# Residual block of two 3x3 convolutions on one core: F(4,3) over ten tiles in two groups, another order of the products, planes made one image further ahead

## What is computed

```python
out = conv3x3(x, lsq_quantize(w1, alpha1))      # pad 1, stride 1, 128 -> 128 channels
out = relu(batchnorm(out, gamma1, beta1))       # mean and variance over batch, rows, columns
out = conv3x3(out, lsq_quantize(w2, alpha2))
out = batchnorm(out, gamma2, beta2)
out = relu(out + x)
```

## Time and profile before

| what | value |
|---|---|
| median of 3 runs | 1474.97 us (1474.01 to 1475.03) |
| the profiled execution: time, span | 1474.11 us, 1472.3 us |
| mean granted TensorE clock | 0.89 |
| PE matmul busy | 1132.3 us, 77% |
| DVE busy | 1145.5 us, 78% |
| ACT busy | 854.4 us, 58% |
| POOL busy | 462.5 us, 31% |

### The profile page before, as it was taken

The page is one execution under the profiler, slowest core; times in us unless marked ns, Lnnn a source line. Parts: engine busy times, 40 slices in busy tenths (PEclk is TensorE's granted clock), DMA queues, the critical chain, the costliest instruction groups (busy, mean ns, idle before and its releaser), DMA issues.

```text
span 1472.3 us, 19175 instructions
## 1 busy us (share of the span) xinstructions
PE 1132.3 (77%) x5802; PEld 1030.9 (70%) x5802; DVE 1145.5 (78%) x1562; ACT 854.4 (58%) x1263; POOL 462.5 (31%) x211
## 2 busy tenths in 40 slices
PE   5999999999999998899999999999999400000000
PEld 5999999999999997899999999999999400000000
DVE  8999999999999996988888888888888642223324
ACT  3655555655565556677777777777777532322224
POOL 3444444444444552433334333333333100000000
PEclk9999999999999999899999999999999755555555
DMA  4454454444452210022245455444230799999999
GB/s 163 157 191 188 189 193 174 174 174 174 174 191 106 96 44 0 0 89 87 93 186 196 184 194 191 179 174 174 87 131 16 277 429 430 431 429 429 430 429 409
DMA packets 28098, 296.83 MB, mean 202 GB/s; under 512 B 3888, under 2 KB 3888, under 8 KB 4912
## 3 DMA queue, kind: packets, MB, share of 16 engines
q1 hardware_dynamic: 22608, 245.25, 42.2%
q10 hardware_dynamic: 5472, 51.38, 8.2%
HBM read 174.59 MB, written 122.03 MB: 201 GB/s over the span
## 4 chain that ended last, share of the span: by engine, by line
issue 52%; POOL 26%; DMA 18%; DVE 1%; ACT 1%; POOLq 1%; ACTq 0%; DVEq 0%
POOL v_lo L417 26%; DMA slots<-conv_spill 11%; DMA out<-slots 4%; DMA xbuf<-in_x 3%; DVE slots L860 1%; ACT slots L611 1%; POOLq L422 1%; POOLq L416 0%; POOLq L77 0%; ACTq L615 0%; POOLq L417 0%; DVE affine L781 0%; DVE tiny L779 0%; DVE affine L782 0%; POOL ident L403 0%
## 5 line engine op out<-in xcount | busy, mean ns | idle before, releaser
L417 POOL TENSOR_TENSOR v_lo<-v_rows,v_hi 128x1008 fp32r<-128x1008 f32 x192 | 460.2, 2429 | 666.8 <-ACT v_hi L469 666.8
L913 PE MATMUL conv_psum<-d_hi,w2T 128*128 128x398 f32 (+2 forms) x864 | 286.6, 336 | 10.3 <-issue 10.3
L913 PE MATMUL conv_psum<-d_hi,w1T 128*128 128x398 f32 (+2 forms) x864 | 286.0, 335 | 2.6 <-ACT slots L488 1.5
L913 PE MATMUL conv_psum<-d_lo,w2T 128*128 128x398 f32 (+2 forms) x864 | 284.9, 334 | 0.0
L913 PE MATMUL conv_psum<-d_lo,w1T 128*128 128x398 f32 (+2 forms) x864 | 284.4, 333 | 0.0
L507 ACT ACTIVATE squares<-slots,minus_shift 128x1008 bf16 (+3 forms) x192 | 225.0, 1172 | 15.0 <-ACT squares L507 12.4
L893 PE MATMUL conv_psum<-v_lo,w1T 128*128 128x512 f32 x576 | 227.2, 394 | 0.0
L893 PE MATMUL conv_psum<-v_lo,w2T 128*128 128x512 f32 x576 | 227.2, 394 | 0.0
L893 PE MATMUL conv_psum<-v_hi,w2T 128*128 128x512 f32 x576 | 226.7, 394 | 0.0
L893 PE MATMUL conv_psum<-v_hi,w1T 128*128 128x512 f32 x576 | 226.6, 393 | 0.0
L860 DVE SCALAR_TENSOR_TENSOR slots<-slots,affine,xbuf 128x3136 f32<-128x3136 f32 (+1 forms) x30 | 97.4, 3265 | 160.9 <-DMA slots<-conv_spill 155.2
(11 more groups left out here) (78 smaller groups left out, 1457.5 us busy)
## 6 DMA issues: line engine op xcount, KB each, us to landing
conv_spill<-slots SPq DMA_DIRECT2D x44, 1568.0 KB, 6.1
slots<-conv_spill SPq DMA_DIRECT2D x44, 1568.0 KB, 10.8
slots<-in_x SPq DMA_DIRECT2D x31, 1568.0 KB, 8.9
out<-slots ACTq DMA_DIRECT2D x30, 1568.0 KB, 11.7
xbuf<-in_x SPq DMA_DIRECT2D x28, 1568.0 KB, 52.9
xbuf_w<-in_x SPq DMA_DIRECT2D x4, 1568.0 KB, 49.9
out<-slots ACTq DMA_DIRECT2D x4, 784.0 KB, 10.3
slots<-in_L_conv_w SPq DMA_DIRECT2D x2, 576.0 KB, 9.7
```

The lines of the kernel that those rows point to most:

```text
L417: nc.gpsimd.tensor_tensor(pair_window(1, k), pair_rows(k), pair_window(0, k).bitcast(F32), ALU.subtract).then_inc(pool_lo_ready, 1)
L913: last = nc.tensor.matmul(bank_run(CHUNK_BANK[j], r1 - r0), w[:, kh * 3 + kw, :], run(d_plane[half], r0 - WINO + 1, r1 - WINO + 1, kw - 1) ...
```

## The change

The Winograd part grows from nine to ten tiles (40 rows), in two groups of five, each group in a bank of its own. A product is now 12 matmuls of 284 columns into two banks; VectorE's and ScalarE's operations on a product read both banks in one instruction of 2 x 284 elements, but the rows of output are written by one instruction a group (280 elements). The direct part shrinks to 16 rows in two chunks of 8 rows (456 and, at the lower edge, 398 columns). Eight banks are shared out anew: products 0 to 3 use banks 2-3, 4-5, 6-7, 0-1; the two outer products use 4-5 and 6-7; the chunks 2 and 3.

TensorE's order becomes: products 0 to 3 of image g, the chunks of image g+1, the two outer products of image g. VectorE makes the planes of image g+2 while image g is finished; the outer pair of image g+1 is made in the same step. The planes are split into three pairs with a semaphore each. SyncE's waits follow the new counters.

```diff
+    GROUPS = 2
+    G_TILES = 5
+    TILES = GROUPS * G_TILES
-    CHUNKS = [(36, 43), (43, 50), (50, 56)]
+    CHUNKS = [(40, 48), (48, 56)]
-    M_BANK = range(M)
-    CHUNK_BANK = [6, 7, 6]
+    QUAD = 4
+    M_BANK = [2, 4, 6, 0, 4, 6]
+    CHUNK_BANK = [2, 3]
...
         # POOL
-                with pool.Fori(k * IMAGES, (k + 1) * IMAGES) as g:
-                    lo_of_pairs(g)
+                lo_of_pair(k * IMAGES, 0)
+                lo_of_pair(k * IMAGES, 1)
+                with pool.Fori(k * IMAGES, (k + 1) * IMAGES - 1) as g:
+                    lo_of_pair(g, 2)
+                    lo_of_pair(g + 1, 0)
+                    lo_of_pair(g + 1, 1)
+                lo_of_pair((k + 1) * IMAGES - 1, 2)
...
         # ACT, step
+                take_m(g, 0)
+                hi_pair(g, 2)
                 if not last:
-                    input_ready()
-                    hi_direct(g + 1, p + 1)
-                take_chunk(g, p, b, NC - 1)
-                take_m(g, 0)
...
+                    hi_pair(g + 1, 0)
                 take_m(g, 1)
                 if not first:
-                    square(g - 1, p + (SLOTS - 1), 1 - b, phase, 1)
                     square(g - 1, p + (SLOTS - 1), 1 - b, phase, 2)
                 if not last:
-                    hi_pairs(g + 1)
+                    hi_pair(g + 1, 1)
                 if relu_next is not None:
                     relu_next()
...
+                    take_chunk(g + 1, p + 1, 1 - b, 0)
+                square(g, p, b, phase, 1)
+                if not last:
+                    take_chunk(g + 1, p + 1, 1 - b, 1)
+                    if input_ready is not None:
+                        input_ready()
+                        hi_direct(g + 2, p + 2)
+                    square(g + 1, p + 1, 1 - b, phase, 0)
...
         # DVE
+            def make_front(g, p, between=None):
                 at_least(v_ready, g * PAIRS)
                 stt(q_rows[:, :], ...).then_inc(qp_ready, 1)
+                dve.wait_ge(qp_ready, g * 2 + 1)
+                at_least(lo_ready[0], g)
+                nc.vector.tensor_tensor(v[0], q_of(2), q_of(1), ALU.add)
+                nc.vector.tensor_tensor(v[1], q_of(2), q_of(1), ALU.subtract).then_inc(v_ready, 1)
+                if between is not None:
+                    between()
                 nc.vector.tensor_tensor(p_rows..., ALU.subtract).then_inc(qp_ready, 1)
                 dve.wait_ge(qp_ready, g * 2 + 2)
+                at_least(lo_ready[1], g)
                 stt(v[2], p_of(0), 2.0, p_of(1))
                 stt(v[3], p_of(0), -2.0, p_of(1)).then_inc(v_ready, 1)
...
             def second_difference(g):
                 dve.wait_ge(m_copied, g * 2 + 2)
-                dve.wait_ge(m_done, g * M + 4)
-                nc.vector.tensor_tensor(m3_bank, rows_of(m3[:, :]), m4, ALU.subtract).then_inc(sums_ready, 1)
+                dve.wait_ge(m_done, g * QUAD + 4)
+                nc.vector.tensor_tensor(m3_banks, grouped(m3[:, :]), m4, ALU.subtract).then_inc(sums_ready, 1)
                 dve.wait_ge(sums_ready, g * SR + 3)
-                nc.vector.tensor_tensor(m4, rows_of(m3[:, :]), m4, ALU.add).then_inc(sums_ready, 1)
+                nc.vector.tensor_tensor(m4, grouped(m3[:, :]), m4, ALU.add).then_inc(sums_ready, 1)
...
+            def row(g, p, b, r, bank, scalar, in1, ready):
+                for grp in range(GROUPS):
+                    ...
+                    nc.vector.scalar_tensor_tensor(out=every_fourth(p, r)[:, grp, :, :], ...,
+                                                   accum_out=sums[b][:, col:col + 1]).then_inc(ready, 1)
+            def inner_rows(g, p, b):
+                row(g, p, b, 1, M_BANK[2], 2.0, d1, rows_ready)
+                dve.wait_ge(sums_ready, g * SR + 4)
+                row(g, p, b, 2, M_BANK[3], 4.0, s1, rows_ready)
+                dve.wait_ge(rows_ready, g * RR + RR)
+                stt(s, m4, 1.0, s).then_inc(sums_ready, 1)
+                stt(d, m3_banks, 8.0, d).then_inc(sums_ready, 1)
+            def outer_row(g, p, b, j):
+                dve.wait_ge(outer_done, g * OD + (j + 1))
+                dve.wait_ge(sums_ready, g * SR + (SR - 1 + j))
+                row(g, p, b, (0, 3)[j], M_BANK[QUAD + j], 1.0, (s1, d1)[j], outer_rows_ready)
...
+            def step(g, p, b, phase, first=False, last=False, input_ready=None):
+                first_difference(g)
+                second_difference(g)
+                inner_rows(g, p, b)
+                if not first and not last:
+                    add_totals(g - 1, 1 - b, phase)
+                if not last:
+                    make_outer(g + 1)
                 if input_ready is not None:
                     input_ready()
+                    make_front(g + 2, p + 2, lambda: outer_row(g, p, b, 0))
+                    lo_direct(g + 2, p + 2)
+                else:
+                    outer_row(g, p, b, 0)
+                outer_row(g, p, b, 1)
...
         # PE
+            def inner_products(g, w):
+                for k in range(QUAD):
+                    if k == 0:
+                        pe.wait_ge(lo_ready[0], g + 1)
+                        pe.wait_ge(evac_done, g * NC + NC)
+                    if k == 2:
+                        pe.wait_ge(lo_ready[1], g + 1)
+                    if not first_step:
+                        if k == 1:
+                            pe.wait_ge(outer_rows_ready, g * OR - 2)
+                        if k == 2:
+                            pe.wait_ge(outer_rows_ready, g * OR)
+                        if k == 3:
+                            pe.wait_ge(sums_ready, g * SR)
+                    product(g, w, k).then_inc(m_done, 1)
+            def outer_products(g, w):
+                pe.wait_ge(lo_ready[2], g + 1)
+                for j in range(2):
+                    pe.wait_ge(sums_ready, g * SR + (2, SR)[j])
+                    product(g, w, QUAD + j).then_inc(outer_done, 1)
+            def convolve(g, w):
+                inner_products(g, w)
+                chunks(g + 1, w)
+                outer_products(g, w)
```

More of the change, by code:

```diff
@@ L153, in residual_block @@
         v_ready = sem("v_ready")
[L154 to L156 removed]
+        hi_ready = [sem(f"hi{k}_ready") for k in range(PAIRS)]
+        lo_ready = [sem(f"lo{k}_ready") for k in range(PAIRS)]
+        direct_hi_ready = sem("direct_hi_ready")
+        direct_lo_ready = sem("direct_lo_ready")
         relu_ready = sem("relu_ready")
         m_done = sem("m_done")
+        outer_done = sem("outer_done")
+        outer_rows_ready = sem("outer_rows_ready")
         m_copied = sem("m_copied")
@@ L489, in take_chunk, with square @@
                                      accum_out=sums[b][:, col:col + 1]).then_inc(evac_done, 1)
-            def square(g, p, b, phase, part):
-                if not (isinstance(g, int) and g * NSQ + part == 0):
-                    act.wait_ge(squared, g * NSQ + part)
+            def square(g, p, b, phase, part, last=False):
+                order = g * NSQ + (-1, 1, 2 if last else 3)[part]
+                if part == 0 and isinstance(g, int) and g % IMAGES == 0:
+                    order = g * NSQ
+                if not (isinstance(order, int) and order == 0):
+                    act.wait_ge(squared, order)
                 if part == 0:
                     act.wait_ge(evac_done, g * NC + NC)
-                    y, n = slot(p + SLOTS, WINO, H), (H - WINO) * W
+                    y, n = slot(p + 2 * SLOTS, WINO, H), (H - WINO) * W
                     into = squares[:, 0:n]
                 elif part == 1:
-                    act.wait_ge(rows_ready, g * RR + 2)
+                    act.wait_ge(rows_ready, g * RR + RR)
                     y, n = two_of_four(p + SLOTS, 0, 1), 2 * N
@@ L575, in relu_over @@
                 def relu_over():
-                    act.wait_ge(relu_ready, m * NR + 2 * NR)
-                step(m + IMAGES, m + SPILL, b, 1, first, second, last, relu_over,
-                     None if isinstance(m, int) and m >= IMAGES - 2 else relu_next)
+                    act.wait_ge(relu_ready, m * NR + 3 * NR)
+                step(m + IMAGES, m + SPILL, b, 1, first, last, relu_over if more else None,
+                     relu_next if more else None)
             act.wait_ge(affine_ready, 1)
@@ L728, in add_totals @@
+            def add_totals(g, b, phase, last=False):
+                dve.wait_ge(squared, g * NSQ + (NSQ if last else NSQ + 1))
                 at_least(totalled, g)
@@ L891, in products @@
                     for kw in range(3):
                         for half in range(2):
-                            last = nc.tensor.matmul(bank_run(M_BANK[k], TILES),
+                            r0 = (k % 2) * TILES + grp * G_TILES
+                            last = nc.tensor.matmul(bank_run(M_BANK[k] + grp, G_TILES),
                                                     w[:, M_WEIGHT[k] + kw, :],
```

(11 more changed lines are left out.)

367 lines of the change are left out of this document (169 added, 198 removed).

## The result

The changed kernel takes 1582.62 us (median of 4 runs, 1581.59 to 1582.86), the kernel before 1474.68 beside it (4 runs, 1474.01 to 1475.03). The ratio is 1.0732, interval [1.0715, 1.0749]. The forecast was 1543, range 1500 to 1610: slower as predicted and inside the range, but by 108 us where 69 were worked out.

The account below looks back on a forecast made before the run. TensorE was taken to bound the kernel before, a TensorE-VectorE loop of 18.52 us an image the one after. On 1474.11 us: +34.4, +34.2, +1.4, 0, +2.3, -3.6, sum +68.7, giving 1543 us; range 1500 to 1610.

Parts of the forecast that it names:

- The mechanism: TensorE waits ahead of product 2 for VectorE's last output row, VectorE for product 3; each image takes 18.52 us.
- The wait ahead of product 2: TensorE idle once an image before product 2, until VectorE's last operation of its step: 1.3 to 2.0 us.
- The period: Time between two starts of product 2: 14.34 + 0.52 + 3.20 + 0.28 + 0.18 = 18.52 us.
- Four waits for its own result: VectorE waiting between the second differences, ahead of `s`, after `q_rows`, after `p_rows`: 4 x 0.13 = 0.52 us.
- 31 x 18.52: 31 steps of each phase at the predicted cycle: 574.1 us, +34.4 in phase 1 and +34.2 in phase 2.
- the closed loop: Products 2 and 3 plus VectorE's whole step except the first difference, without overlap: 18.52 us, above TensorE's 16.90.
- The +1.4: First step of phase 1: a wait for image 1's low direct rows before its chunks, +1.4 us.
- The seam: Between the phases: same work a tenth longer, last chunks already gone; 0, bounded at 5 us either way.
- The ends: Start 0; last second difference to last pass +2.3 us; last pass -3.6 us, through earlier residual loads.
- TensorE keeps the pace: Rival: no wait before product 2, TensorE's 16.90 us an image sets the time, 1445 us; chance 0.07.
- GpSimd in ahead: Rival: GpSimd's outer-pair subtraction (2.38 us) beats `lo_direct`, first by 0.8; cycle 21.7, 1741 us; chance 0.07.
- The clock: Rival: TensorE's new 1.6 us gaps lower its clock, products 2 and 3 at 1.2 GHz: 1741 us; chance 0.02.

Follow-up runs that it names:

- reordered kernel: Changed kernel with VectorE making both outer rows and `lo_direct` right after `q_rows`, planes last, and ScalarE's copies and casts reordered: 1464.53 us, 0.9934 of the kernel before.
- the kernel with the early delay: Changed kernel with two reductions of 568 elements (0.66 us each) added on VectorE ahead of `s` and `d`: 1931.91 us (one run).

## Why the prediction was right, and where it was short

**The mechanism was right.** The wait ahead of product 2 is there in every regular image, 1.69 us (stated 1.3 to 2.0), released by VectorE's row; VectorE has its gap ahead of the second difference, 1.93 (stated some 2.2). Moving row 3 one place earlier made the program 17 us faster, moving it away removed that wait, and 0.66 and 1.31 us added to the loop made steps of 19.43 and 20.08 wherever the matmuls kept their pace, which is 18.77 and what was added.

**The period** was 18.77 for 18.52, in both phases. Term by term:

| term | predicted | measured |
|---|---|---|
| product 2's start to second difference (3.20 + 0.28) | 3.48 | 3.44 |
| a row of 280 elements | 0.37 | 0.37 (318.59 to 318.96) |
| `s`, `d`, each | 0.66 | 0.66 to 0.67 |
| totals | 0.13 | 0.07 |
| outer pair of planes to `q_rows` | 1.245 | 1.62 |
| `q_rows`, to the planes | 2.43 + 0.13 | 2.53 |
| end of last row to TensorE | 0.18 | 0.23 (332.24 to 332.47) |

What was too small in the period is the count of VectorE's waits for itself: "Four waits for its own result". There is a fifth, ahead of `q_rows`: `make_front` begins with a wait on `v_ready`, which the outer pair just made has to raise, since both use `q_rows`' buffer. In the kernel before, the pair of planes was followed by work that did not need it. The sum has nothing for this place; it costs 0.38, of which the trace shows 0.30 as idle. Some 0.2 of it stands only in the steps of the loop (`Fori`): in the ten steps of phase 1 that are written out, the pair is followed by `q_rows` after 1.42 and not 1.62 (109.55 to 110.97), and those that are otherwise undisturbed last 18.6 and not 18.77. 62 x 0.38 would be 23 us; the four self-waits at 0.10 to 0.13 instead of 0.13, and the totals, gave some of it back, so that 0.25 x 62 = 15.5 us remain of it. The line with the wait was in the diff.

**The regular period was applied to irregular steps.** "31 x 18.52" left 12 us of phase 1 and 5 of phase 2 out. The second weights, in the diff untouched and hidden before, were not in the sum; what covered them was not named, and the closed loop had left a cover of some 2 us an image, too little for the one operation of 4.27. The runs without them put this at 9.6 us. The rest is image 0's step, where GpSimd and VectorE collide (5.61 for 1.40) and the long gap lowers the clock. The prediction had that mechanism as a rival, with a condition for the regular step alone: there `lo_direct` was in fact ahead, by 0.53 of the 0.8 reckoned. In the first step GpSimd asks 2.1 us earlier after the second difference than in the regular one, and it happened. The +1.4 that the sum has for this step is for another wait, that of the chunks for the low direct rows, which is not there: the chunks start at 37.64, 2.5 us before the second difference.

**The seam** came at +4.7, at the edge of its bound of 5. It has a collision of the same kind (`v_rows` 3.61 at 657.32). **The ends** were +1.3, +3.5 and -2.6 for 0, +2.3 and -3.6.

So of the 39.7 us missing, 15.5 are the size of the period (31 x 0.25 a phase), 15.9 the irregular steps (17.3 less the 1.4 that the sum had), and 8.3 the start, the seam and the ends. The range of 1500 to 1610 was built from the prices of a row and of a self-wait alone, so that it also held the 24 us that came from elsewhere is luck.

**The rivals.** *TensorE keeps the pace* is out for this order of work. Its price was about right: TensorE's own work is 16.8 against the 16.90 reckoned. The reordered kernel comes near that pace, at 17.01. It is at 1464.5 and not 1445, since a difference of 0.11 per image is 7 us and the irregular steps and ends cost the rest. *GpSimd in ahead* has about the right price (2.15 for 2.4); GpSimd did get in in three irregular steps and in the seam, and in the regular steps `lo_direct` was ahead of it by 0.53 us. *The clock* was given the right sign and no trigger: it stayed with a gap of 1.69 us in every image and fell in most images with one of 2.34. The spacing of 284 columns is 0.132 (48 starts from 305.50 to 311.71), as the kernel before had let expect (0.133), and not 0.121.

## What to carry to other kernels

When a change moves the last consumer of a buffer behind another engine's whole step, write down the cycle of waits that it closes and sum both engines' parts of it; an engine can be busy for three quarters of the time and the loop still set the period. Then count each wait of the engine for itself anew in the new order, and price anew everything that was free before because that engine had slack: one-time work, first steps, the engine that shares its inputs. Before giving up the smaller amount of work, try an order that takes the producer of the closing wait forward: here the same tiles went from 7% slower to 0.7% faster by the order of VectorE's and ScalarE's work alone.

## What the runs showed of the hardware that was not expected

- **TensorE's clock and short gaps.** Gaps of 1.69 us, one an image, left the granted clock at 1.00 from 300 to 500 us; with gaps of 2.34 it is 0.94 there, with gaps of 3.0 it is 0.88 and with 4.9 it is 0.85. The slow matmuls are some or all of those right behind the gap, at 0.237 for 284 columns instead of 0.132. Where they close a loop their time is added to the step: 0.66 us added became 0.66 in one step of three and some 2.1 in the others. The gap itself does not grow by it: 1.69 + 0.66 is the 2.35 and 1.69 + 1.31 the 3.00 that the trace has. The time follows the added work more than in proportion (62 x 0.66 = 41 us became 94).
- **GpSimd and VectorE.** VectorE's operation on two SBUF inputs waits for the rest of GpSimd's instruction. In the kernel with row 3 one place earlier, `lo_direct` takes 3.04 where it starts 0.37 after GpSimd and 2.59 where it starts 0.80 after: 0.43 later, 0.45 shorter. With GpSimd's 2.40 alone and its own 1.07, waiting and then working would give 3.10 and 2.67. In the kernel with the early delay it takes 3.30 at 0.66 behind, 0.5 more than that sum; why is not shown. An operation with one SBUF input is held too: L282 takes 0.76 at 8.83, where GpSimd does nothing, and 2.21 at 80.85, 1.14 behind GpSimd's start at 79.71. The rows of output, which read PSUM, are not held (0.44 at 331.50, within GpSimd's 5.21 from 330.97). Which comes first by a fraction of a microsecond decides over 0.7 to 2.2 us per image.
- **VectorE waiting for its own result** costs 0.10 to 0.13 us between two like operations, 0.18 behind the outer pair of planes in the steps that are written out and 0.38 there in the steps of the `Fori` loop. Where these last 0.2 come from stays open.
